# Regrouping one attention output through a scratch tensor: row order of the scratch, and one read or sixteen

## The reference, cut to what matters

```python
Q = Q.reshape(B, T_src, N_HEADS, D_HEAD).transpose(0, 2, 1, 3)     # 16 heads of 16
...
scores = jax.nn.softmax(dot, axis=-1)
out = jnp.einsum('bhst,bhtd->bhsd', scores, V)
out = out.reshape(B, T_src, D_MODEL)
return out @ Wh.T + bh
```

## Time and profile before

| | before |
|---|---|
| median of three runs | 1033.23 us |
| profiled execution | 1029.88 us |
| its span | 1028.2 us |
| PE busy | 875.7 us (85%) |
| ACT, DVE, POOL busy | 547.9, 495.9, 117.2 us |
| mean granted clock of PE | 0.927 |
| PE waiting for the regrouped `y` (four times) | 18.6 us in three batches, 6.9 us in the last |

### The profile page before, as it was taken

One profiled execution on the slowest core, in us unless ns is written; L12 is line 12 of the kernel. 1 busy time (PEld: TensorE's weight loads), 2 busy tenths in 40 slices (PEclk: granted clock), 3 DMA queues, 4 the chain that ended last, 5 costly groups with the idle time before them and its releaser, 6 DMA issues.

```text
span 1028.2 us, 20422 instructions
## 1 busy us (share of the span) xinstructions
PE 875.7 (85%) x8611; PEld 605.9 (59%) x8611; DVE 495.9 (48%) x831; ACT 547.9 (53%) x597; POOL 117.2 (11%) x132
## 2 busy tenths in 40 slices
PE   4697998996899997897899997897899999944855
PEld 3465665665566665665566665665566666632644
DVE  6532235463544446763544446763544444524546
ACT  6175777673466664664466664654466665720101
POOL 1052000000411000000411000000421000004300
PEclk9698999998999998998999998998999998976887
DMA  5999988995666666756766666747666665020000
GB/s 168 157 206 235 154 177 155 165 152 122 125 124 124 124 123 104 128 110 124 134 124 122 123 104 125 124 105 134 123 123 109 121 112 73 2 42 0 1 1 13
DMA packets 59281, 117.99 MB, mean 115 GB/s; under 512 B 23152, under 2 KB 30320, under 8 KB 55728
## 3 DMA queue, kind: packets, MB, share of 16 engines
q1 hardware_dynamic: 57392, 112.22, 59.5%
q0 software_dynamic: 1792, 4.40, 1.5%
HBM read 78.84 MB, written 37.75 MB: 113 GB/s over the span
## 4 chain that ended last, share of the span: by engine, by line
PE 63%; DVE 11%; DMA 11%; issue 5%; ACT 4%; POOL 2%; DVEq 2%; SPq 1%; POOLq 0%; ACTq 0%
PE ps_o L709 16%; PE ps_s L721 11%; PE ps_p L534 8%; PE ps_p L567 8%; DMA kscr<-kparts 4%; DMA ctx_raw<-ctxT 3%; ACT probs L988 3%; DMA oscr<-y 3%; PE ps_a L660 2%; PE ps_a L654 2%; PE ps_a L686 2%; PE ps_a L597 2%; DVE ctx_lo L1013 1%; PE ps_a L673 1%; DVE kfeat L1233 1%
## 5 line engine op out<-in xcount | busy, mean ns | idle before, releaser
L988 ACT ACTIVATE probs<-ps_s 128x1024 f32<-128x1024 f32 x512 | 497.0, 1023 | 294.6 <-PE ps_s L721 267.4
L709 PE MATMUL ps_o<-probs,values 128*17 128x256 f32 x4096 | 250.1, 384 | 0.0
L721 PE MATMUL ps_s<-qstack,kstack 64*128 64x256 f32 x2048 | 199.0, 310 | 19.9 <-ACT probs L988 13.4
L721 PEld LDWEIGHTS ps_s<-qstack,kstack 64*128 64x128 f32 x2048 | 141.6, 188 | 109.8 <-ACT probs L988 57.6
L709 PEld LDWEIGHTS ps_o<-probs,values 128*17 128x17 f32 x4096 | 108.1, 98 | 98.8 <-issue 9.6
L1042 DVE TENSOR_TENSOR values<-ps_p,bv_pair 128x512 f32<-128x512 f32 x64 | 44.2, 691 | 100.7 <-PE ps_p L567 100.6
L534 PE MATMUL ps_p<-ctx_hi,wk_hi 128*128 128x512 f32 x128 | 62.5, 488 | 31.5 <-DVE ctx_lo L1013 25.4
L1025 DVE TENSOR_SCALAR kparts<-ps_p,b_heads 128x512 fp32r<-128x512 f32 x64 | 48.1, 751 | 81.1 <-PE ps_p L534 73.2
L567 PE MATMUL ps_p<-wv_hi,ctx_hi 128*128 128x256 f32 x256 | 81.2, 317 | 3.2 <-DVE wv_lo L1013 3.2
L963 ACT ACTIVATE feat<-feat,node_neg 128x512 f32<-128x512 f32 x32 | 23.1, 722 | 105.4 <-DVE feat L1217 105.4
L567 PE MATMUL ps_p<-wv_hi,ctx_lo 128*128 128x256 f32 x256 | 74.6, 292 | 1.2 <-issue 1.2
(11 more groups left out here) (209 smaller groups left out, 995.5 us busy)
## 6 DMA issues: line engine op xcount, KB each, us to landing
kstack<-kscr SPq DMA_DIRECT2D x192, 256.0 KB, 9.4
kscr<-kparts SPq DMA_DIRECT2D x64, 512.0 KB, 8.3
ctx_raw<-ctxT SPq DMA_DIRECT2D x32, 512.0 KB, 13.5
qstack<-qscr SPq DMA_DIRECT2D x24, 128.0 KB, 5.2
qscr<-qparts SPq DMA_DIRECT2D x4, 512.0 KB, 3.2
xh<-x SPq DMA_DIRECT2D x4, 256.0 KB, 11.5
xs<-x SPq DMA_DIRECT2D x4, 256.0 KB, 13.8
oscr<-y SPq DMA_DIRECT2D x8, 128.0 KB, 7.2
```

The source lines that it names most:

```text
L709: last = mm(ps_o[32 * j:32 * j + DH + 1, g * S:(g + 1) * S], values[par][:, i, head_of_step(g, j), :], prob[:, j * S:(j + 1) * S], start=b ...
L721: last = mm(ps_s[s % 2][:, j * S:(j + 1) * S], kstack[par][rows, u, i * P:(i + 1) * P], queries[rows, u, :], start=True, stop=True)
L988: nc.scalar.activation(probs[n % AHEAD][:, :], ps_s[n % 2][:, :], ACT.Exp, scale=float(DH) ** -0.5).then_inc(fast["exp_done"], 1)
```

## The change

The scratch tensor changes its order from head, position, dimension to position, head, dimension. Each of the two writes then copies 128 whole rows of 1 KB and no longer cuts each row into 16 pieces of 64 bytes. The read back has to pick the pieces instead: sixteen transfers, one for each head, each of which fills the 16 partitions that belong to that head, with 16 pieces of 64 bytes for each partition. The semaphore value for which `yT` waits is multiplied by the number of heads. The same functions serve a second, general path of the program that is entered only when a sum of exponentials is out of range; it has the same edit.

```diff
-        oscr = scratch("oscr", [H, S, DH], FP32)
+        oscr = scratch("oscr", [S, H, DH], FP32)
...
                 for t in range(ST):
-                    sp.dma_start(oscr[:, t * P:(t + 1) * P, :].rearrange("h s d -> s h d"),
-                                 y[:, t, :].rearrange("p (h d) -> p h d", h=H)).then_inc(c["o_written"], 16)
+                    sp.dma_start(oscr[t * P:(t + 1) * P, :, :].rearrange("s h d -> s (h d)"),
+                                 y[:, t, :]).then_inc(c["o_written"], 16)
 
             def regroup_output(c, tails):
 
                 wait_all((c["o_written"], tails * 32 + 32))
-                sp.dma_start(y[:, :, :], oscr.rearrange("(t a) (u s) d -> (a u) t (s d)", t=ST, u=S // DH)
-                             ).then_inc(c["o_in"], 16)
+                for h in range(H):
+                    row = h % HALF * DH
+                    sp.dma_start(y[row:row + DH, h // HALF, :].rearrange("u (s d) -> u s d", d=DH),
+                                 oscr[:, h, :].rearrange("(u s) d -> u s d", s=DH)).then_inc(c["o_in"], 16)
...
                 elif name == "yT":
-                    pe.wait_ge(c["o_in"], clock[1] * 16 + 16)
+                    pe.wait_ge(c["o_in"], (clock[1] * 16 + 16) * H)
```

## The result

The changed kernel took 1062.59 us (median of four runs, 1058.71 to 1062.76) against 1032.05 for the kernel before: ratio 1.029, 95% interval [1.0262, 1.0318]. A second comparison gave 1060.94 against 1033.27: 1.0274 [1.0244, 1.0304]. The change makes the kernel 2.7 to 2.9% slower, 28 to 31 us. The forecast had the direction right, but it was 10.4 us, a third of the loss, and its range ended at 1054.

The account below looks back on a forecast made before the run. PE, 63% of the chain, waits for regrouped y at four places. Longer reads less faster writes give +2.35 us in each of three batches and +3.4 last, +10.4 on 1033.23: 1043.5 us, range 1036.5 to 1054.

Parts of the forecast that it names:

- the signs set down beforehand: Regrouping: issues near 0.42 us, writes landed in 2.1 us (end) and 5.3 us (batch 2), PE idle about 8 us.
- Reads, pitch: Sixteen read issues on SP, one each 0.44 us (0.35 to 0.465), so the sixteenth starts 6.6 us behind the first.
- Reads, last landing and first issue: After the sixteenth read issue starts, its data land 1.9 us later (1.7 to 3.0); read phase 8.5 us in all.
- Writes: Whole-row writes of y land earlier: gains of 3.1, 3.1 and 3.0 us in batches 1 to 3, 2.4 us last.
- The reading of the windows: In batches 1 to 3, the second write is let in only when the slowest engines finish the first's 128 pieces, 1.5 us.
- Nothing behind it: On SP behind the reads, write_keys moves from 479.1 to 482.6 us but stays hidden, with 4.3 us to spare.
- Counting nothing for the clock: PE's clock already falls during the stall, so no cost was added; a shifted recovery would be about 1 us a batch.
- Rival A: The 64-byte reads are slow, 45 ns a piece: read phase 13.0 us, +28.4 in all, 1062 us; chance 0.12.
- issues longer than 0.6 us: Sign at the sixteen reads on SP that would prove the forecast wrong and point to Rival A.
- the DMA share: Sign during the regrouping's reads: a share near 1 would prove the forecast wrong and point to Rival A.
- an estimate of 26 ns for the worst heads: Reads of heads off a 256-byte boundary: 11 units against 5, so 26 ns a piece, just under the 27 that stays hidden.

Follow-up runs that it names:

- two queues: The changed kernel with eight of its sixteen reads issued by ACT and the other eight by SP: 1040.87 us, ratio 1.0097.
- eight and thirty-two reads: The changed kernel with the same 4096 pieces read in eight transfers of two heads, or thirty-two of half a head: 1042.57 us and 1077.94 us.
- The turned order: The kernel before, with SP issuing the regrouping's writes and read ahead of the loads of ctx_raw and xs in pass 0: 1020.18 us, ratio 0.9888.
- its turned order: The changed kernel with SP issuing the regrouping's writes and reads ahead of the loads of ctx_raw and xs in pass 0: 1052.96 us, ratio 1.018.
- the row writes alone: The changed kernel with one plain read of 1 KB rows, so pieces are not regrouped and the output differs: 1021.55 us, ratio 0.991.

## Why the prediction was wrong

The direction, the place and the mechanism held: PE waits for the last piece at all four places; the writes give, the reads take, nothing else joins in. The sum failed in one term above all. Of the signs set down beforehand, the writes landed as said at the end (2.2 us for 2.1) and nearly so in batch 2 (5.75 for 5.3), but the issues took 0.61 us and not 0.42, and PE stood idle for 12.2 us and not 8.

- **Reads, pitch: mis-sized.** Forecast 0.44 us from forms of the trace (0.35 to 0.465), measured 0.65: 15 x 0.21 x 4 = 12.6 us of the 15.4 by which the traced loss (25.8) exceeds the forecast (10.4). The step that failed is the transfer of `kstack`'s 0.42 us to the new form, and the claim that the median of 0.42 us plus the gap (0.465) is the upper bound. The trace of before had no transfer of this pattern. That the issue is the bound is shown (two queues, eight and thirty-two reads, a DMA share of 0.27), and that the form sets its price is shown in place (0.448 against 0.608 us). Why the chip takes longer for that form is open.
- **Reads, last landing and first issue: a little short.** 1.9 us forecast, 12.1 - 15 x 0.65 = 2.35 measured: 1.8 us over four places. With the 1.1 us that the writes gave less, the three terms come to 15.5.
- **Writes: about right.** Gains of 3.7, 2.6, 2.0 and 2.3 us at the four places, 10.5 in all against 11.6. The reading of the windows, that the second write stood behind the first one's 128 small pieces on the slowest engines, fits but was not tested by itself; the packets of the trace agree with it: in batch 2 half of the 4096 small pieces had started by 476.0 us, the last of them at a trickle of 9 GB/s, and the other half followed at once. The turned order shows that the loads ahead were worth 10 us, which the prediction took as given and did not look into.
- **Nothing behind it: right.** `write_keys` moved back, the next `stack_keys` still issued on the scores' end, and behind the four places no wait for `kstack` or `kscr` is new. Counting nothing for the clock was right too: from a read's landing to the next `y` the three stretches changed by -1.0, -0.6 and -0.2 us, and the end by +0.6.
- **What the traced regroupings leave.** The forecast missed the medians by 20.1 us in the first comparison and by 17.3 in the second. Beside the 15.4, in the first, 3.0 us lie in the common stretches (the first `y` 4.1 us later, the others 1.2 us shorter) and 1.7 between profiled executions and medians. No term of the sum stands for them. The late first `y` is not shown to be part of the change: in the two kernels with test transfers, which are the changed kernel up to its last store, it came at 235.6 and 240.4 us.
- **Rival A gave 1062 us, and for the wrong reason: its closeness is luck.** It had the DMA engines take 45 ns a piece and pace the queue at 0.72 us. The pace was near that (0.65); its cause was the issue, doubling the pieces of a transfer did not slow it, and a piece took 11 ns at most. So "issues longer than 0.6 us" was a poor sign of A; the DMA share, which A wanted near 1 and which was 0.27, told the two apart. The prediction also had an estimate of 26 ns for the worst heads, worked out from what the Trainium skill states of pieces that don't start on a 256-byte boundary (page "DMA: Bandwidth & Descriptors", section "How a descriptor splits into AXI transactions"). The trace does not bear it out: 16 such pieces would fill 0.64 of a window of 0.65 us, and one head in four would have them, but the windows between 939.7 and 950.1 us show 0.22 to 0.33, and the share follows the bytes moved.
- **The range was too narrow for its own reasoning.** The pitch was bounded by other forms and the upper bound set at the median of the nearest. A price that the trace doesn't show had no upper bound there, and fifteen issues at four places multiply every error by sixty.

## What to carry to other kernels

A few transfers with many small pieces can beat many small transfers: count the issues that stand one behind another between a landing and the engine that waits, and multiply the price of one by all of them. Take that price from a transfer with the same pattern, or measure it in a row of test transfers first. And look at what stands ahead of a late transfer in its queue: turning two loads behind it was worth about as much as the row writes alone (11.5 us against 9.2), and needed no change of layout.

## What the runs showed of the hardware that was not expected

- An issue on SP cost 0.42 to 0.46 us for 1 to 24 pieces of 64 bytes for each of 16 partitions where they leave a rest of the pitch between partitions, and 0.61 to 0.63 us for 16, 32 and (32 partitions) 8 where they fill it. At 16 pieces that was so for loads and stores alike and for pieces of 32 to 128 bytes. 64 partitions x 3 pieces are the exception.
- An issue can keep SP for long behind transfers that are still moving: the second write's took 4.3 to 6.5 us in the batches of the kernel before and 0.87 us in the last. With whole rows it took 0.44 us at most in the changed kernel, but 1.80 and 1.54 us in batches 2 and 3 of its turned order, so small pieces are not the only condition.
- Two queues issued such transfers side by side without slowing each other (0.61 and 0.63 us).
- Reads of 64-byte pieces from device memory took the DMA engines 11 ns a piece at most (24.6% of 16 engines for 11.5 us, 4096 pieces), whichever head's 64 bytes of the 1 KB row they were; the 1 KB pieces of the old read took 45 ns at 365 GB/s.
